# The convolution's fourth tap moves to ScalarE, the norms' roots too, and a 14th product to GpSimd

## The reference

```
n  = layernorm(x)
a  = rmsnorm(n) @ W_in                 -> xs (512), res (512)
xs = silu(conv4(xs) + conv_b)          # causal, depthwise, 4 taps
dt, B, C = split(xs @ W_x);  dt = softplus(dt @ W_dt)
h  = exp(A * dt) * h + dt * xs * B     # over time, 512 channels x 16 states
y  = sum over the states of h * C
x  = x + n + (y * silu(res)) @ W_out
m  = layernorm(x)                      # expert e takes rows 512e to 512e+511
out = x + (silu(m @ w1[e]) * (m @ w3[e])) @ w2[e]
```

## Time and profile before

| | |
|---|---|
| profiled execution, its time | 1013.09 us |
| its span | 1011.3 us |
| VectorE busy | 923.8 us (91%) |
| GpSimd busy | 909.1 us (90%) |
| TensorE busy | 924.9 us (91%) |
| ScalarE busy | 697.0 us (69%) |
| mean granted TensorE clock | 0.973 |

### The profile page before, as it was taken

One profiled execution on the slowest core, in us unless ns is written; L12 is line 12 of the kernel. 1 busy time (PEld: TensorE's weight loads), 2 busy tenths in 40 slices (PEclk: granted clock), 3 DMA queues, 4 the chain that ended last, 5 costly groups with the idle time before them and its releaser, 6 DMA issues.

```text
span 1011.3 us, 13001 instructions
## 1 busy us (share of the span) xinstructions
PE 924.9 (91%) x4160; PEld 591.8 (59%) x4160; DVE 923.8 (91%) x1003; ACT 697.0 (69%) x1188; POOL 909.1 (90%) x499
## 2 busy tenths in 40 slices
PE   6888978999999999999999999999999997669978
PEld 4445545655756556655756557655656655555745
DVE  5789889999999999999999999999999999899941
ACT  4556777778758877778758867687758876567610
POOL 1499899999999999999999999999999999999910
PEclk9999998999999999999999999999999999779989
DMA  5590135010841039010851039110750028100200
GB/s 170 198 348 21 42 131 246 1 65 3 329 172 43 24 129 372 2 66 0 312 190 42 25 112 343 47 65 1 288 214 25 21 99 320 42 21 1 87 22 21
DMA packets 42852, 117.86 MB, mean 117 GB/s; under 512 B 8608, under 2 KB 27040, under 8 KB 32672
## 3 DMA queue, kind: packets, MB, share of 16 engines
q1 hardware_dynamic: 40928, 116.99, 30.9%
q10 hardware_dynamic: 1856, 0.04, 0.1%
HBM read 110.21 MB, written 6.82 MB: 116 GB/s over the span
## 4 chain that ended last, share of the span: by engine, by line
DVE 35%; issue 18%; PE 11%; POOL 10%; ACT 9%; DVEq 0%; POOLq 0%; ACTq 0%
DVE ring L664 24%; DVE ring L649 8%; POOL hc L513 7%; PE gbank L1070 4%; PE gbank L1084 3%; POOL ring L499 3%; ACT ebank L806 2%; PE ybank L1133 2%; ACT hb L1008 1%; DVE dt_ L629 1%; ACT L1011 1%; ACT L1004 1%; PE gbank L1194 1%; DVE hb L753 1%; DVE sres L676 1%
## 5 line engine op out<-in xcount | busy, mean ns | idle before, releaser
L664 DVE TENSOR_TENSOR_SCAN ring<-ebank,state,ring 128x512 f32<-128x512 f32 x512 | 623.5, 1267 | 28.0 <-ACT ebank L806 19.7
L513 POOL TENSOR_TENSOR hc<-ring,c_all 128x1024 f32<-128x1024 f32 x255 | 599.0, 2368 | 22.6 <-DMA c_all<-bc_kept 11.0
L806 ACT ACTIVATE ebank<-dt_,a_neg 128x512 f32<-128x512 f32 x512 | 349.6, 689 | 218.5 <-DVE ring L664 216.7
L1133 PEld LDWEIGHTS ybank<-ident,hc 128*128 128x128 f32 x2048 | 236.8, 143 | 105.2 <-issue 62.8
L1133 PE MATMUL ybank<-ident,hc 128*128 128x128 f32 x2048 | 262.0, 277 | 24.7 <-POOL hc L513 12.4
L499 POOL TENSOR_TENSOR ring<-b_all,u 128x1024 f32<-128x1024 f32 x103 | 243.9, 2368 | 2.3 <-ACT state L810 2.3
L649 DVE TENSOR_TENSOR ring<-b_all,ubank 128x1024 f32<-128x1024 f32 x151 | 180.5, 1195 | 1.7 <-ACT ubank L820 1.7
L1070 PE MATMUL gbank<-xT,w 128*128 128x512 f32 x320 | 150.7, 605 | 12.3 <-DVE hb L753 11.4
L1070 PE MATMUL gbank<-xT,w_a 128*128 128x512 f32 x256 | 118.5, 601 | 6.2 <-DVE dt_ L629 4.0
L1070 PE MATMUL gbank<-xs,w_a 128*128 128x512 f32 x224 | 101.0, 595 | 0.0
L1070 PEld LDWEIGHTS gbank<-xT,w 128*128 128x128 f32 x320 | 57.1, 193 | 64.5 <-issue 51.5
(11 more groups left out here) (135 smaller groups left out, 752.1 us busy)
## 6 DMA issues: line engine op xcount, KB each, us to landing
b_all<-bc_kept SPq DMA_DIRECT2D x32, 1024.0 KB, 7.2
c_all<-bc_kept SPq DMA_DIRECT2D x32, 1024.0 KB, 8.3
w<-in_L_ffn_w_dram SPq DMA_DIRECT2D x16, 640.0 KB, 4.9
w_a<-wc_kept SPq DMA_DIRECT2D x7, 1024.0 KB, 4.8
w_a<-win_kept SPq DMA_DIRECT2D x6, 1024.0 KB, 8.9
w2s<-in_L_ffn_w_dram SPq DMA_DIRECT2D x8, 640.0 KB, 4.5
xin<-in_L_attn_x_dram SPq DMA_DIRECT2D x9, 512.0 KB, 3.5
x<-in_L_attn_x_dram SPq DMA_DIRECT2D x7, 512.0 KB, 7.2
```

The source lines that it names most:

```text
L513: ch_ok.by(e.tensor_tensor(hc[:, q % HC, :, :], ring[:, q % RING, :, :], c_all[:, n:n + NG, :], ALU.mult))
L664: h_ok.by(e.tensor_tensor_scan(row, ebank[j % 2][:, :], row, initial=state[:, q, n:n + 1], op0=ALU.mult, op1=ALU.add))
L806: e_ok.by(e.activation(ebank[j % 2][:, :], dt_[:, d, :], ACT.Exp, scale=a_neg[:, d, k:k + 1]))
L1133: last = e.matmul(ybank[:, cols(b)], hc[:, q % HC, n, cols(b)], ident[:, :], is_transpose=True, start=(k == 0 and n == 0 and b == 0), stop ...
```

## The change

- Convolution: `before_conv` now makes two instructions of each bank: the copy to `xpre`, and a copy of the bank onto itself, scaled by the fourth tap. TensorE adds the three other taps to that bank instead of filling a second one, so a bank is held from `IN` until the convolution is read. VectorE's `convolved` is gone; ScalarE's `convolved` copies the bank to `xs`.
- Norms: ScalarE makes the roots (`rooted`: Ln, Ln, Copy, Exp, Identity; `rooted2`: Ln, Copy, Exp). GpSimd keeps one product for each norm. `hand_on` is gone; the scales of three chunks are kept in `st`.
- GpSimd makes 14 products of B and u in a chunk instead of 13, partly at other tiles.
- `silus_res` is gone from iteration 0; its SiLU of 128x2048 is done in `silus` of iteration 1, and iteration 0 has one SiLU stretch.
- The steps of many jobs move by one to three in all tables.

```diff
-    POOL_BU = (1, 4, 6, 7, 10, 12, 15, 18, 19, 22, 25, 26, 29)
+    POOL_BU = (1, 4, 7, 10, 11, 14, 16, 18, 21, 22, 23, 24, 26, 29)
...
                     out_at[b] = i * Q + until
+                    if name == "IN" and i >= 0:
+                        made[b] += 1
+                        PLACE[of, "CV", k] = b, made[b]
+                        out_at[b] = i * Q + added[k]
...
             def front(c, i):                                   # GpSimd
...
-                scales.by(e.tensor_tensor(st[:, 4, :], m, minus, ALU.mult))
-                scales.by(e.tensor_scalar(st[:, 0, :], v, 1.0 + EPS, EPS * EPS, ALU.mult, ALU.add))
-                scales.by(e.tensor_scalar(st[:, 1, :], v, 1.0, EPS, ALU.mult, ALU.add))
-                scales.wait(e, c, 3)
-                scales.by(e.tensor_tensor(st[:, 2:4, :], st[:, 0:2, :], mhalf, ALU.pow))
-                scales.wait(e, c, 4)
-                scales.by(e.tensor_tensor(st[:, 5:7, :], st[:, 2:4, :], ..., ALU.mult))
-                scales.by(e.tensor_scalar(st[:, 7, :], st[:, 3, :], 1.0, 1.0, ALU.mult, ALU.add))
+                roots.wait(e, c, 4)
+                xn_ok.wait(e, c - 1)
+                x1a_ok.wait(e, c - 3)
+                mine = st[:, c % 3, :, :]
+                scales.by(e.tensor_tensor(mine[:, 3:7:3, :], mine[:, 4:8:3, :], ..., ALU.mult))
...
             def back(c, i):                                    # GpSimd
-                stats2.wait(e, c)
+                roots2.wait(e, c)
                 xn2_ok.wait(e, c - 1)
-                scales2.by(e.tensor_tensor(st2[:, 2, :], mv2[:, :, 0], minus, ALU.mult))
-                scales2.by(e.tensor_scalar(st2[:, 0, :], mv2[:, :, 1], 1.0, EPS, ALU.mult, ALU.add))
-                scales2.wait(e, c, 2)
-                scales2.by(e.tensor_tensor(st2[:, 1, :], st2[:, 0, :], mhalf[:, 0, :], ALU.pow))
-                scales2.wait(e, c, 3)
                 scales2.by(e.tensor_tensor(st2[:, 3, :], st2[:, 2, :], st2[:, 1, :], ALU.mult))
...
+            def rooted(c, i):                                  # ScalarE
+                stats.wait(e, c)
+                scales.wait(e, c - 1)
+                x1a_ok.wait(e, c - 3)
+                mine, eps, eps2 = st[:, c % 3, :, :], consts[:, 0, 0:1], consts[:, 1, 0:1]
+                roots.by(e.activation(mine[:, 0, :], mv[:, :, 1], ACT.Ln, scale=1.0 + EPS, bias=eps2))
+                roots.by(e.activation(mine[:, 1, :], mv[:, :, 1], ACT.Ln, bias=eps))
+                roots.by(e.activation(mine[:, 2, :], mv[:, :, 0], ACT.Copy, scale=-1.0))
+                roots.wait(e, c, 2)
+                roots.by(e.activation(mine[:, 4:8:3, :], mine[:, 0:2, :], ACT.Exp, scale=-0.5))
+                roots.wait(e, c, 4)
+                roots.by(e.activation(mine[:, 5, :], mine[:, 7, :], ACT.Identity, bias=1.0))
...
-                        move("IN", d, i, xpre[:, d, HALO:HALO + TC])
+                        bank = wait_full(e, i, "IN", d)
+                        e.activation(xpre[:, d, HALO:HALO + TC], bank[:, :], ACT.Copy)
+                        read_out(e.activation(bank[:, :], bank[:, :], ACT.Copy, scale=cw[:, d, HALO:TAPS]), i, "IN", d)
+            def convolved(d):                                  # ScalarE
+                def job(c, i):
+                    u_ok.wait(e, c - 1, d + 1)
+                    move("CV", d, i, xs[:, d, :])
...
             def silus(c, i):
...
                 xs_silus(c, i)
-                e.preload_act_table_set(LOG_EXP)
-            def silus_res(c, i):
-                e.preload_act_table(ACT.Silu)
-                res_silu(c, i)
+                if i == 1:
+                    res_silu(c - 1, i - 1)
                 e.preload_act_table_set(LOG_EXP)
...
+            def rooted2(c, i):                                 # ScalarE
+                stats2.wait(e, c)
+                scales2.wait(e, c - 1)
+                xn2_ok.wait(e, c - 1)
+                roots2.by(e.activation(st2[:, 0, :], mv2[:, :, 1], ACT.Ln, bias=consts[:, 0, 0:1]))
+                roots2.by(e.activation(st2[:, 2, :], mv2[:, :, 0], ACT.Copy, scale=-1.0))
+                roots2.wait(e, c, 1)
+                roots2.by(e.activation(st2[:, 1, :], st2[:, 0, :], ACT.Exp, scale=-0.5))
...
-                    bank = wait_free(e, i, "CV", d)            # TensorE
-                    filled(product(bank[:, :], [(cdiag[:, d, k, :], xpre[:, d, k:k + TC]) for k in range(TAPS - 1)]), i, "CV", d)
+                    bank = gbank[PLACE[i, "CV", d][0]]
+                    filled(add_on(bank[:, :], [(cdiag[:, d, k, :], xpre[:, d, k:k + TC]) for k in range(TAPS - 1)]), i, "CV", d)
```

More of the change, by code:

```diff
@@ L118, in mamba_moe_layer @@
[L118 to L122, removed]
@@ L124, in mamba_moe_layer @@
+            (24, "back", "DOWN", 0, 29.2), (27, "back", "DOWN", 1, 32.3), (28, "front", "DT", 3, 32.4),
+            (29, "scan y", "YT", 2, 31.4), (31, "next", "XT", 0, 31.6)]
         SETUP = [
@@ L771, in _ @@
             first_u()
-            table = [(3, "front", convolved(0)), (4, "back", gated(ND - 1)), (4, "front", convolved(1)),
-                     (6, "front", convolved(2)), (6, "front", convolved(3)), (8, "back", m_stats), (14, "scan", gated(0)),
-                     (17, "front", dt_of(0)), (20, "next", x_stats), (20, "scan", gated(1)), (20, "back", hidden(0)),
-                     (20, "back", hidden(1)), (20, "back", hidden_tail), (21, "back", hidden(2)), (22, "back", hidden(3)),
-                     (23, "back", hidden(4)), (24, "front", dt_of(1)), (27, "front", dt_of(2)), (28, "ahead y", gated(2)),
-                     (30, "scan y", gated(2)), (31, "front", dt_of(ND - 1))]
@@ L1044, in _ @@
             normal(1, -1)
-            table = [(1, "front", before_conv(0, 1)), (2, "front", before_conv(2, 3)), (3, "back", y_read(ND - 1)),
-                     (6, "back", residual), (8, "front", silus), (9, "back", m_copy), (10, "scan", y_read(0)),
-                     (11, "front", res(0, 1)), (12, "front", res(2, 3)), (13, "back", normal2), (13, "front", bc_read),
-                     (14, "back", turned("OXT")), (16, "front", softplus(0)), (17, "back", gate(0, 1)), (18, "back", gate(2, 3)),
-                     (18, "scan", y_read(1)), (19, "back", gate(4)), (20, "back", tails), (20, "back", gate_silus),
-                     (23, "front", softplus(1)), (26, "ahead y", y_read(2)), (27, "front", softplus(2)),
-                     (27, "scan y", y_read(2)), (28, "front", softplus(ND - 1)), (30, "next", normal), (31, "next", turned("XT"))]
@@ L1052, in _ @@
[L1052 to L1061 removed]
+            table = [(2, "front", before_conv(0, 1)), (2, "back", y_read(ND - 1)), (2, "front", before_conv(2, 3)),
+                     (3, "front", convolved(0)), (4, "front", convolved(1)), (5, "back", residual), (6, "front", convolved(2)),
+                     (6, "front", convolved(3)), (8, "front", silus), (9, "back", rooted2), (9, "back", m_copy),
+                     (10, "scan", y_read(0)), (11, "front", res(0, 1)), (12, "back", normal2), (13, "front", res(2, 3)),
+                     (13, "front", bc_read), (14, "back", turned("OXT")), (16, "front", softplus(0)), (17, "back", gate(0, 1)),
+                     (18, "back", gate(2, 3)), (18, "scan", y_read(1)), (19, "back", gate(4)), (19, "back", tails),
+                     (20, "back", gate_silus), (22, "next", rooted), (25, "front", softplus(1)), (26, "ahead y", y_read(2)),
+                     (26, "front", softplus(2)), (27, "scan y", y_read(2)), (29, "next", normal), (30, "front", softplus(ND - 1)),
+                     (31, "next", turned("XT"))]
@@ new lines, in _ @@
+            table += [(24, "back", down_on(0)), (25, "back", down_on(1)), (28, "ahead", residual), (29, "back", down_out(0)),
+                      (31, "back", down_out(1))]
+            last = [(1, "back", y_last), (3, "back", scales_last), (4, "back", turned_last), (7, "back", silus_last)]
+            table0 = [(0, "scan", first_u), (1, "late", wc_first_part), (4, "late", softplus(1)), (4, "late", wc_rest(1)),
+                      (4, "late", wc_rest(2)), (5, "late", softplus(2)), (8, "late", res(0, 1)), (9, "late", softplus(3)),
+                      (11, "late", res(2, 3)), (11, "late x", turned("XT")), (13, "scan", y_read(0)),
+                      (14, "front", before_conv(0, 1)), (15, "front", convolved(0)), (15, "front", before_conv(2, 3)),
+                      (17, "front", convolved(1)), (18, "front", convolved(2)), (18, "front", convolved(3)),
+                      (19, "front", silus_first), (20, "scan", y_read(1)), (20, "front", res(0, 1)), (22, "front", res(2, 3)),
+                      (22, "next", rooted), (23, "front", bc_read), (24, "front", softplus(0)), (26, "front", softplus(1)),
+                      (27, "scan", y_read(2)), (28, "front", softplus(2)), (28, "next", normal), (30, "front", softplus(ND - 1)),
```

141 lines of the change are left out of this document (60 added, 81 removed), and 6 rows, old and new, of the table FIRST.

## The result

The changed kernel takes 1019.08 us (median of 15 runs, 1017.35 to 1023.64); the kernel before, run beside it, 1015.12 us (15 runs, 1012.59 to 1017.65). The ratio is 1.0047, 95% interval 1.0033 to 1.006: slower. Single runs of the kernel before lie near 1013, 1015 and 1017.5 us, with mean granted clocks of about 0.973, 0.969 and 0.968, so that the 1012.83 us of the first three runs was its lower end. The prediction, 1001 us in a range of 990 to 1010 and faster with a chance of 0.88, was wrong.

A forecast was written before the change was run, and what follows sets the result against it. VectorE and GpSimd, both full in a 114.5 us beat, were taken as the bound. Gains of 5.5 us (first beat), 6.0 (six full beats) and 0.8 (last), 12.3 in sum, took 1013.09 to 1000.8, said as 1001 us; range 990 to 1010.

The forecast's parts named there:

- Step 2: Full beat, `before_conv` and `y_read` together: 5.0 us of ScalarE work in 3.2 us of room, a new 1.7 us wait.
- step 20: Full beat, `gate_silus`: tile 21's product no longer covers it, so VectorE's wait grows from 0.7 to 1.1 to 1.3 us.
- step 29: Full beat, `normal` and `down_out`: 2.5 us of ScalarE work against 2.1 us of room, a wait of 0.4 us.
- Steps 8 and 9: Full beat, VectorE's waits behind `silus` (about 0.2 us) and behind `rooted2` and `m_copy` (0.7 us).
- Step 8: Full beat, `silus`: `m_stats` ahead of the scans lengthens ScalarE's lead; wait about 0.2 us instead of 0.46.
- First beat: The 127.2 us beat of iteration 0: 5.5 us gained, bounds 2 and 9, from 4.4 + 4.0 + 0.9 - 3.8.
- The 4.4 us for `silus_res`: First beat: VectorE's 4.4 us wait for exps at `silus_res` goes, as that 4.5 us ScalarE stretch is removed.
- The last beat and the end: Last beat of 110.3 us: 0.8 us gained; the end of 48.0 us: 0.
- W_in late: Rival: W_in's reload, issued later, holds up `IN` 0; 1019 us at 2 us lost a beat; chance 0.09 with the like.
- GpSimd's floor: Rival: the new ScalarE stretches hide and GpSimd's 112.3 us sets the full beat; 991.5 us, chance 0.26.
- ScalarE eats it: Rival: each stretch leaves 0.4 us more behind, waits of 5.5 us, full beats gain nothing; 1010.5 us, chance 0.13.
- the moved SiLU: First of the six full beats: the SiLU from iteration 0 adds 1.8 us to `silus`, without new cover.

The follow-up runs named there:

- a_mst8: Changed kernel with `m_stats` back at step 8 instead of 7: 1006.81 us, ratio 0.9916 to the kernel before.
- a_tap2: Changed kernel with the oldest of TensorE's three convolution taps not computed: 1007.62 us, ratio 0.9924 to the kernel before.
- a_warm: Changed kernel with `UP` 1's product made twice, to fill TensorE's wait ahead of `UP` 2: 1013.60 us, ratio 0.9989 to the kernel before.
- b_roots: Kernel before with the norms' part of the change alone, tiles as before: 1021.83 us, ratio 1.0062 to the kernel before.
- b_rwarm: b_roots with `UP` 1's product made twice: 1014.71 us, ratio 0.999 to the kernel before.
- b_warm: Kernel before with `UP` 1's product made twice: 1017.17 us, ratio 1.0018 to the kernel before.
- b_silu: Kernel before without `silus_res` in iteration 0, its SiLU in `silus` of iteration 1: 1017.19 us, ratio 1.0016 to the kernel before.
- m8_bc1: a_mst8 with the first `before_conv` back in a stretch of its own at step 1: 1002.79 us, ratio 0.9877 to the kernel before.
- b_tap2: Kernel before with the oldest of TensorE's convolution taps not computed: 1025.01 us, ratio 1.0097 to the kernel before.

## Why the prediction was wrong, by its steps

**Busy times and prices: right.** VectorE was to have 108.6 us in a full beat and has 109.1; GpSimd about 112.3, 112.0; ScalarE 93.7, 92.7. The copy of a bank onto itself, bounded by 0.55 and 0.69 us, took 0.677, and the copy to `xs` 0.598 (ScalarE's groups over the whole span: busy us, mean ns, idle before):

```profile
L833 ACT ACTIVATE gbank<-gbank,cw 128x512 f32<-128x512 f32 x28 | 19.0, 677 | 0.0
L795 ACT ACTIVATE xs<-gbank 128x512 f32<-128x512 f32 x28 | 16.7, 598 | 0.4 <-PE gbank L1084 0.2
```

**The walk through the table: right but for one step, and that step decided it.** Step 2's wait was to be 1.7 us and is 1.59; step 20's 1.1 to 1.3, is 1.4 (in two); step 29's 0.4, is 0.45. Steps 8 and 9 together were to cost 0.9 us; in the changed kernel the wait at M swallows them, and in a_mst8, without it, they cost 0.62 (0.46 and 0.16). Step 8 failed: "`m_stats` now lies ahead of step 8's scans, which gives ScalarE a longer lead". I counted what the earlier `m_stats` gives to ScalarE and didn't ask whether its input was there. M's second half is made at 29.9 us into the beat, the job now begins at 27.0, has read the first half at 27.8, and VectorE stands 2.2 us. With the job back at its step the beats are 113.3 us; the forecast was 113.2. That M's lateness is the cause of these 1.5 us a beat is shown from both ends: a later `m_stats` (a_mst8) and an earlier M (a_tap2) give the same beat.

**The error under it.** "TensorE's 111.6 us is a modelled figure, and I don't take it for a limit." In the trace of before, its matmul instructions follow each other at 0.4275 us (512 columns), 0.215 (256) and 0.1075 (128) at the full clock; 508 of them in a beat are 108.0 us by these intervals. Waits are 2.9 us, and 3.4 us are left over between groups, of the beat's 114.3. It was as full as the two engines I looked at. It isn't the bound (a_tap2), but a full engine's results come when they come, and no step of the prediction looked at when.

**The clock: in no rival.** The sum was made at one speed. The change shifted TensorE's waits a little (1.9 to 2.1 us at `UP` 2, 1.7 to 2.1 before), and four of six beats instead of one paid 1.7 us. Filling the wait takes the stretches away: 5.5 us in a_warm, 7 us between b_roots and b_rwarm. So the wait at `UP` 2 is needed for these stretches; what decides in a single beat isn't shown: in after, waits of 2.10 and 2.08 us were followed by full speed, 1.89 and 2.08 by half clock. Before's median lies 2.3 us above the 1012.83 us from which the sum was checked; by b_warm, with a median of 1017.17 us, this wait can't be all of the reason.

The Trainium skill (page "TensorE: Matmul & The Clock Gate", section "HAM oscillation — how this bites in real kernels") describes this pattern, a wait in every pass of a loop behind which the clock falls every time, and advises to restructure the loop so that TensorE stays warm. The trace agrees in part, with 7.11 us against 5.42 behind such a wait: here the wait is for VectorE and not for a DMA, and the clock falls behind it in four of six beats, not in all.

**First beat: a third term off.** 5.5 us were forecast, 2.7 came. The 4.4 us for `silus_res` were a wait that another one mostly replaces (b_silu: 0.7 us lost, or some 0.9 gained by the estimate above). VectorE's waits for exps fell only from 11.5 to 9.2 us, and two others grew: for GpSimd's products from 1.7 to 3.9 us, and of `dt_`, behind a late `softplus`, from 1.5 to 2.7 us. First the changed kernel, then the two rows of before:

```profile
DVE ring L637 <- ACT ebank L776: 9.2, 7, 2.6
DVE ring L637 <- POOL ring L487: 3.9, 4, 2.8
DVE dt_ L611 <- ACT xpre L901: 2.7, 1, 2.7
```

```profile
DVE ring L664 <- POOL ring L499: 1.7, 2, 1.0
DVE dt_ L629 <- ACT xpre L912: 1.5, 1, 1.5
```

**The last beat and the end.** 0.8 us were forecast for the last beat, 0.1 came; the end of 48.0 us grew by 1.1 where 0 was forecast. Neither was looked into.

**The rivals.** W_in late, which gave 1019 us, didn't occur: no `IN` 0 of a full beat waits for it. The reload was issued later than forecast, 106 to 108 us into the beat instead of 101, but it lands faster than in the earlier trace rows:

```profile
w_a<-win_kept SPq DMA_DIRECT2D x6, 1024.0 KB, 4.8
```

It landed at 391.71 us and `IN` 0 began at 394.67. With the 8.9 us of the earlier trace rows it would have landed some 1.1 us too late (an estimate from these rows), so the margin was thinner than the prediction had it. The time is that rival's by accident; its mechanism isn't there. GpSimd's floor set the beat in no profiled version of the changed kernel; m8_bc1 comes nearest, with 0.7 us of idle time left. "ScalarE eats it" is in part what the first beat did, not the full ones.

**The account.** Forecast 12.3 us gained; got 6.4 lost in the profiled executions. Of the 18.7 us the wait at M has 9.3 (114.85 less 113.3, six times), the clock 5.1 (three stretches more), the first beat 2.8, the last beat and the end 1.8, and the start gave 0.3. That these add up is in part luck: the forecast had 1.8 us for the moved SiLU, which the wait at M hid, and against that 113.3 us is 0.1 over the forecast's 113.2, and its 114.5 us for before is 0.2 over five of the six beats and leaves out the half-clock stretch in the sixth.

Not tried: the convolution's part alone on before, and the change's 14 products alone.

## What to carry to other kernels

Before a job is moved one step earlier, find the instant at which its input is made on the other engine, and compare it with the instant at which the job will ask; the table's order says nothing of it. Here 3.4 us earlier was 2.2 us too early. Sum up TensorE's matmul intervals and its waits against the beat even where its busy time is modelled, and treat an engine that fills the beat as a source of lateness, whether or not it bounds. Where TensorE has one wait of about 2 us in each beat, a change elsewhere can set off the lower clock behind it and cost more than it brings: read the granted clock beat by beat, and try filling the wait with a repeated product.

## What the hardware showed that I had not expected

- Work added sped the kernel up (1.7 us of repeated matmuls a beat, 5.5 us gained in a_warm), and work taken away slowed it (3.4 us less on TensorE a beat, 10 us lost in b_tap2). In both the granted clock differs behind TensorE's longest wait; for a_warm the filled wait shows it, for b_tap2 (7.7 us in its six full beats) only the trace does, since no run filled its wait.
- A half-clock stretch costs about 1.7 us of the beat where dense matmuls stand in it (5.42 to 7.11 us in after; 114.3 to 115.9 in before), and 1.3 us in b_roots (115.85 against 114.55 in b_rwarm).
- ScalarE may read and write the same bank of PSUM in one scaled copy: 677 ns for 128x512, some 80 ns over a plain copy to SBUF (598) and 10 under a scaled one (687).
